# Attention on one Trainium2 core: five PSUM banks for scores split 2 + 3 in place of 3 + 2

## The reference, cut to what matters

```python
attn = jnp.einsum('bhqd,bhkd->bhqk', q, k) * scale
attn = jnp.where(causal, attn, -jnp.inf)       # first layer
m = jnp.max(attn, axis=-1, keepdims=True)      # clipped to +-100 in the first layer
e = jnp.exp(attn - m)
p = e / jnp.sum(e, axis=-1, keepdims=True)     # with a floor of 1e-8 in the first layer
out = jnp.einsum('bhqk,bhkd->bhqd', p, v)
```

## Time and profile before

| | |
|---|---|
| median of 3 runs | 2695.88 us (2695.67 to 2700.51) |
| the profiled execution | 2708.65 us, of which the profile's span is 2706.9 us |
| mean granted TensorE clock | 0.963 |
| PE busy | 2469.7 us, 91% of the span |
| DVE busy | 1834.3 us, 68% |
| ACT busy | 1437.0 us, 53% |
| POOL busy | 1344.7 us, 50% |
| attention stretches (slots of elements 0 to 7, 8 to 15, 16 to 23) | 73 to 634 us, 639 to 1164 us, 1891 to 2407 us |

### The profile page before, as it was taken

One profiled execution on the slowest core, in us unless ns is written; L12 is line 12 of the kernel. 1 busy time (PEld: TensorE's weight loads), 2 busy tenths in 40 slices (PEclk: granted clock), 3 DMA queues, 4 the chain that ended last, 5 costly groups with the idle time before them and its releaser, 6 DMA issues. The chain is left out here.

```text
span 2706.9 us, 46628 instructions
## 1 busy us (share of the span) xinstructions
PE 2469.7 (91%) x15144; PEld 1428.9 (53%) x15144; DVE 1834.3 (68%) x3670; ACT 1437.0 (53%) x2991; POOL 1344.7 (50%) x1359
## 2 busy tenths in 40 slices
PE   4999999999999999989994899976999999989997
PEld 2455555554444444368894466652344444349896
DVE  3899999998778887833333566755778888844333
ACT  2666666666777777643331222102777777653332
POOL 4466555653345554246453466633335555445554
PEclk8999999999999999999997799986999999999998
DMA  5333333333434444146554000004334444335553
GB/s 149 88 107 106 99 97 106 114 114 91 120 119 130 131 125 115 48 145 195 185 194 146 0 1 16 16 31 123 107 113 129 131 130 123 91 113 176 188 200 115
DMA packets 250018, 306.35 MB, mean 113 GB/s; under 512 B 27692, under 2 KB 224945, under 8 KB 249780
## 3 DMA queue, kind: packets, MB, share of 16 engines
q1 hardware_dynamic: 239604, 277.11, 34.2%
q0 software_dynamic: 10176, 26.27, 2.7%
HBM read 210.85 MB, written 92.84 MB: 112 GB/s over the span
## 5 line engine op out<-in xcount | busy, mean ns | idle before, releaser
L698 DVE TENSOR_REDUCE neg_max_af<-sc_af 128x1 f32<-128x512 f32 (+3 forms) x864 | 550.8, 664 | 122.0 <-PE sc_af L414 86.2
L628 ACT ACTIVATE prob_af<-sct_af 128x512 f32<-128x512 f32 (+1 forms) x864 | 484.9, 582 | 253.7 <-PE sct_af L435 139.8
L698 DVE TENSOR_REDUCE neg_max_f<-sc_f 128x1 f32<-128x512 f32 x512 | 334.3, 685 | 102.7 <-PE sc_f L414 100.0
L628 ACT ACTIVATE prob_f<-sct_f 128x512 f32<-128x512 f32 x512 | 291.4, 598 | 143.0 <-PE sct_f L435 140.4
L414 PE MATMUL sc_af<-stack_k_af,stack_q_af 96*128 96x512 bf16 (+3 forms) x1024 | 333.0, 345 | 15.5 <-DVE neg_max_af L698 15.1
L435 PE MATMUL sct_af<-stack_q_af,stack_k_af 99*128 99x512 bf16 (+3 forms) x1024 | 331.2, 345 | 6.8 <-ACT prob_af L628 5.4
L1513 PE MATMUL hT_ps_e<-xT_e,w_r 128*128 128x128 f32 x2240 | 266.6, 278 | 5.1 <-DMA w_r<-in_f_W_dram 4.0
L1513 PEld LDWEIGHTS hT_ps_e<-xT_e,w_r 128*128 128x128 f32 x2240 | 264.4, 194 | 10.7 <-DMA w_r<-in_f_W_dram 6.0
L1500 PE MATMUL y_ps_e<-w_r,hT_e 128*128 x1120 | 256.5, 382 | 5.9 <-issue 3.8
L727 DVE SCALAR_TENSOR_TENSOR prob_af<-prob_af,w_r 128x512 f32<-128x512 f32 (+2 forms) x224 | 234.3, 1054 | 25.4 <-ACT prob_af L628 25.3
L466 PE MATMUL out_af<-prob_af,v_aug_af 128*32 128x512 f32 (+3 forms) x2048 | 231.8, 524 | 7.2 <-DVE prob_af L727 6.3
(11 more groups left out here) (358 smaller groups left out, 4658.3 us busy)
## 6 DMA issues: line engine op xcount, KB each, us to landing
w_r<-in_f_W_dram SPq DMA_DIRECT2D x78, 1024.0 KB, 6.3
k_parts_d<-parts_af SPq DMA_DIRECT2D x192, 128.0 KB
stack_k_af<-k_parts_d SPq DMA_DIRECT2D x64, 384.0 KB, 4.3
q_parts_d<-parts_af SPq DMA_DIRECT2D x96, 128.0 KB
stack_q_af<-q_parts_d SPq DMA_DIRECT2D x64, 192.0 KB, 3.0
k_parts_d<-parts_f SPq DMA_DIRECT2D x96, 128.0 KB
stack_k_f<-k_parts_d SPq DMA_DIRECT2D x32, 384.0 KB, 4.3
xt_r<-sorted_x SPq DMA_DIRECT2D x70, 128.5 KB
```

Source lines behind the costliest of these rows:

```text
L628: nc.scalar.activation(dst, src.rearrange("p (h q) -> p h q", h=len(heads)), ACT.Exp).then_inc(S.exp_done, 1)
L698: nc.vector.tensor_reduce(M.neg_max[:, qt, heads[0]:heads[-1] + 1], src, AX.X, ALU.max, negate=True).then_inc(S.max_done, 1)
```

## The change

One bank goes from `sc` to `sct`. `M.sc` has two banks and `M.sct` three; the index is u % 2 for `sc` and u % 3 for `sct` at every place where PE writes or DVE and ACT read. With it the waits change: unit u of `sc` waits for the maximum of unit u - 2 (before: u - 3), unit u of `sct` for the exponential of unit u - 3 (before: u - 2). `floor_row` shares the `sct` banks. No instruction is added, removed or moved on any engine: the five streams list the same instructions in the same order, and the only differences are the counts that PE waits for, and which of the first units of each kind wait at all.

```diff
@@ score
-                if u >= 3:
-                    pe.wait_ge(S.max_done, u - 2)
-                bank = M.sc[u % 3]
+                if u >= 2:
+                    pe.wait_ge(S.max_done, u - 1)
+                bank = M.sc[u % 2]
@@ score_t (floor_row alike)
-                if u >= 2:
-                    pe.wait_ge(S.exp_done, u - 1)
-                bank = M.sct[u % 2]
+                if u >= 3:
+                    pe.wait_ge(S.exp_done, u - 2)
+                bank = M.sct[u % 3]
@@ exp (floor_exp alike)
-                src = M.sct[u % 2][:, 0:len(heads) * cols]
+                src = M.sct[u % 3][:, 0:len(heads) * cols]
@@ row_max
-                src = M.sc[u % 3][:, 0:len(heads) * cols].rearrange("p (h k) -> p h k", h=len(heads))
+                src = M.sc[u % 2][:, 0:len(heads) * cols].rearrange("p (h k) -> p h k", h=len(heads))
@@ attention_memory
-    M.sc = [psum("sc0"), psum("sc1"), psum("sc2")]
-    M.sct = [psum("sct0"), psum("sct1")]
+    M.sc = [psum("sc0"), psum("sc1")]
+    M.sct = [psum("sct0"), psum("sct1"), psum("sct2")]
```

More of the change, by code:

```diff
@@ L446, in floor_row @@
                 u = floor_unit(n, g, i)
-                if u >= 2:
-                    pe.wait_ge(S.exp_done, u - 1)
-                nc.tensor.matmul(M.sct[u % 2][:, :], M.stack_k[96:99, g, i, 0:P], M.stack_q[96:99, g, i, :],
+                if u >= 3:
+                    pe.wait_ge(S.exp_done, u - 2)
+                nc.tensor.matmul(M.sct[u % 3][:, :], M.stack_k[96:99, g, i, 0:P], M.stack_q[96:99, g, i, :],
                                  start=True, stop=True).then_inc(S.t_ps, 1)
@@ L634, in floor_exp @@
                     act.wait_ge(S.pv_done, pv_count(n, g, 0) - 1 - KT)
-                nc.scalar.activation(M.floor[:, g % 2, i, :], M.sct[u % 2][:, :], ACT.Exp, bias=C.minus100[:, 0:1]).then_inc(S.exp_done, 1)
+                nc.scalar.activation(M.floor[:, g % 2, i, :], M.sct[u % 3][:, :], ACT.Exp, bias=C.minus100[:, 0:1]).then_inc(S.exp_done, 1)
             def slot(n, g, kt):
```

## The result

| | before | changed | |
|---|---|---|---|
| median | 2696.74 us (2695.67 to 2700.51) | 2783.44 us (2766.89 to 2785.3) | +86.7 us |
| ratio | 1 | 1.0305, 95% interval 1.0264 to 1.0346 | slower by 3% |
| profiled execution | 2708.65 us | 2785.3 us | +76.7 us |

The kernel is slower, as forecast, and its median lies inside the range, 37 us above the likeliest value of 2746 us. The two profiled executions differ by 76.7 us where 50 had been worked out. The other 10 us of the difference of medians is that the profiled execution of before was 12 us above its own median; further runs of the kernel before gave 2691.66 to 2709.98 us.

What follows compares the result with a forecast made beforehand. PE was taken to bound the attention stretches. Added waits of 55 us, less 8 given back, plus 3.4 for the clock, made 50 us on 2695.9: 2746 us, range 2712 to 2795 us.

Steps and rivals of the forecast that it cites:

- The bound and the direction: In the three attention stretches, 1602 us together, PE is the bound and what it stands still is lost.
- The waits, place by place: Added `score` waits for late maxima in slots 11, 15, 0, 3, 7 and the causal elements: 55 us.
- What the third bank gives back: Waits for exponentials in causal slot 0 and the last groups of elements 15 and 23: 8 us of at most 20.
- The clock: Two more causal elements get a stretch at 1.2 GHz behind slot 3: 3.4 us; nothing counted in other stretches.
- The freed waits win: Late maxima only replace existing PE pauses and 20 us of exponential waits go: 2676 us; faster 0.05.
- The delays add up: DVE runs dry and its lateness returns at each next place, 158 us less 8: 2846 us; above 2795 us 0.08.
- Nothing: Waits in the attention stretches only trade places one to one, time stays 2696 us; chance 0.04.
- The clock falls in slot 11 too: Stretches at 1.2 GHz in slot 11, 12 times, plus all causal elements: 2770 us; 0.15 shared with partial adding up.
- What would show it: Profile signs: `score` waits 10 to 30 us or more (639 to 1164 us), PE share down 3 points, ordinary slots unchanged.

Runs made afterwards that it cites:

- the two filled kernels: Changed kernel with added matmuls in slot 11 and causal slot 3: 2754.51 us; kernel before with 8 added matmuls in causal slot 3: 2692.98 us.
- two banks and two: Two sc banks as in the changed kernel, two sct banks as before, one bank left unused: 2783.72 us, ratio 1.0282 to before.

## Why the prediction was right, and what it had too small

**The bound and the direction.** PE is the bound and its pauses are lost time. Right: with 4.2 us more in each ordinary plain element, nothing behind it gave any back.

**The waits, place by place.** The sum had 55 us for them, less 8 that the third `sct` bank gives back: 47 us. With the clock up on both sides the stretches and the opening grew by 51 us. That the totals are so close is in part luck: the sizes were right, but the counts were not, and the errors made up for one another. In the ordinary plain elements each size came out to 0.02 us (slots 0, 3, 7, 11, 15). But slot 11 stands behind `choose` in 10 elements and not 12, which makes 12.2 us and not 14.8; the 0.55 us of slot 15 came in 10 elements and not 16, the 0.41 us of slot 0 in 10 and not 14, the 0.22 us of slot 3 in 12 and not 16. In the causal elements, where 2.4 us each had been worked out, elements 1 to 6 lost 1.3 to 1.4 us, read from the two filled kernels: slot 2 lost 0.18 us and not 0.43, slot 3 0.76 and not 0.98, slot 5 got shorter by 0.45 us, since its `pv` no longer waits for a clip, so an old pause did swallow a part of the shift there, slots 7, 11 and 15 lost 0.28, 0.35 and 0.28, as worked out. The difference came back in places that had no term of their own: slots 3 and 4 of element 15 took 1.0 and 1.9 us longer in the filled kernel than in the kernel before, the last causal element 2.8 us, the opening 3.1 us.

**What the third bank gives back.** 8 us forecast, 5 to 6 us measured. The reading that `pv` stands behind the same exponential was right in kind: of the 0.63 us in slot 10 of element 15 0.49 went, more than the 0.35 I had read, and in slots 9 and 13 nothing. Many of the smaller waits had no slot that got shorter by them.

**The clock.** This is the term that was mis-sized: 3.4 us in the sum, some 25 us in the runs (76.7 - 51 = 26 in the profiles; 86.7 - 61.5 = 25 in the medians of the unfilled and the filled pair, or 21 by their ratios). The 29 us that filling wins in the changed kernel are more than this term, since the kernel before has slow stretches too. In the causal layer I let two more elements fall, each by one stretch of 3.4 us; in the profiled execution of the changed kernel elements 1 to 7 fell, by 6.8 us. In slot 11 I counted nothing, because a pause of 1.6 us had never brought a slow stretch there. But the changed kernel pauses 2.07 us and, one pair of matmuls later, 0.78 us more, and then it did in seven elements. The step that failed is the inference from a pause that had done no harm to a longer one. I had this as a rival, with 2770 us and 0.15 with its neighbour, and it is the case that came in, with the causal layer in addition. What the Trainium skill tells in TensorE: Matmul & The Clock Gate, "A second HAM failure mode: psum-queue depth-cycling" bears on it: it tells of a kernel whose clock goes up and down because PE pauses shortly between its groups of matmuls while it goes round its PSUM banks. The trace agrees in part. The clock did not fall in every slot, but behind the long pauses only (slot 3 of the causal elements, slot 11 of the plain ones, and some places of the irregular elements 0, 7, 15 and 23); the small waits of slots 0, 3, 7 and 15 left it at 1.00.

**The rivals.** *The freed waits win*: refuted, the freed waits are 5 to 6 us. *The delays add up*: refuted, in elements 9 to 13 and 17 to 21 every slot without a late maximum kept its length to 0.02 us. *Nothing*: refuted. (The chances as listed leave 0.08 above the range, not 0.07.) *The clock falls in slot 11 too*: confirmed by filling the pause.

**What would show it.** The waits of `score` were to grow from about 10 to 30 us or more; they grew to 20.5 us by the profile's count, which leaves out 0.16 us at each, so to 25 us at the most. PE's busy share was to fall by some 3 points and fell by 1.6 to 2, among other things since PE at 1.2 GHz counts as busy (3.40 of 3.40 us in the window of 859.60). Both signs were set too high. The other signs were there, except that the stretch behind the last layer's attention and the one in between varied by some us by themselves.

## What to carry to other kernels

In this kernel the third bank belongs to the side whose reader has the most irregular programme, not to the side that waits most often: DVE, with a chain of 3 us of other work between two maxima, needed its third bank, and ACT could do with two. What such a bank is worth can be worked out from one trace, by setting the start of each write beside the end of the read that would then guard it and carrying the shift on from place to place; but pauses on TensorE have to be priced twice, once by their length and once by the clock behind them, and a pause that did no harm says nothing of a longer one. If a pause can't be avoided, cut up the other engine's long piece of work first, and fill the rest with matmuls.

## What the runs showed of the hardware that I had not expected

- Adding 26 matmuls of 128 bf16 columns to a pause of 2 us made the slot 1.5 to 1.6 us shorter (8.44 to 6.86 us), since the clock stayed at its upper level. With the causal pauses filled too, the whole kernel won 29 us (2783.44 to 2754.51 us).
- Executions of one program spend different amounts of time at 1.2 GHz in the same stretch: in 593 us of the causal layer 58 us, in another execution with the same instructions in that stretch 14 us, and the stretch was 19 us shorter. Where an expected difference is of that size, the medians can't tell it (two banks and two against the changed kernel: 2783.72 and 2783.44 us), while the slots of the traces, which agree to 0.02 us where the clock is up, can.
- In the causal layer a slow stretch followed pauses of twice 0.57 us in four elements of eight, and in the plain layers none followed a single pause of 1.5 to 1.6 us in eight. In the changed kernel slot 11 of element 18 has the same two pauses as that of element 10 (2.07 and 0.78 us) and no slow stretch. How long the pause is does not decide alone; what does, these runs leave open.
